# GpSimd waits for each group's own gathers in three stages of a graph network

## The reference

```python
# attention layer (twice): 8 heads of 16, then 1 head of 64
e = leaky_relu(xl[src] + xr[dst], 0.2)
logits = einsum('ehc,hc->eh', e, att)
m = segment_max(logits, dst, num_segments=N)
...
# third layer
pos_e = x_feat[src] + edge_attr
v = gelu(pos_e @ W1.T + b1, approximate=False) * bases
aggr = segment_sum(v, dst, num_segments=n_nodes)
```

## Time and profile before

| | us |
|---|---|
| median of 3 runs | 6841.29 |
| lowest and highest run | 6835.71, 6842.03 |
| span of the profiled execution | 8166.8 |

### The profile page before, as it was taken

How to read it: one execution, slowest core, us unless ns; L and a number is a source line. 1 busy time by engine, 2 the same in 40 slices (tenths; PEclk the granted TensorE clock), 3 DMA queues, 4 the chain that set the end, 5 groups by cost and what they waited for, 6 DMA issues and landing times. The chain is left out here.

```text
span 8166.8 us, 113382 instructions
## 1 busy us (share of the span) xinstructions
PE 6013.4 (74%) x30494; PEld 4713.9 (58%) x30494; DVE 3761.8 (46%) x13003; ACT 2160.8 (26%) x7007; POOL 4622.4 (57%) x4391
## 2 busy tenths in 40 slices
PE   3788878646766888876686887455555689989898
PEld 2666766535665666655575887355555544544545
DVE  5344443148973444311688335344555543333333
ACT  3222222228852222222697002111111220000000
POOL 2555555567865555555786552666666436366363
PEclk8666666768976666677898999677777789999999
DMA  5566654356642333323444664444444557867777
GB/s 202 180 188 207 206 177 130 109 93 142 140 78 69 79 77 80 73 61 60 63 76 73 238 228 154 116 128 126 127 128 127 107 178 261 291 230 265 262 263 239
DMA packets 904017, 1231.57 MB, mean 151 GB/s; under 512 B 230601, under 2 KB 640861, under 8 KB 890407
## 3 DMA queue, kind: packets, MB, share of 16 engines
q1 hardware_dynamic: 607544, 887.00, 34.1%
q0 software_dynamic: 207392, 219.55, 14.4%
q10 hardware_dynamic: 88428, 117.57, 4.2%
HBM read 987.45 MB, written 237.38 MB: 150 GB/s over the span
## 5 line engine op out<-in xcount | busy, mean ns | idle before, releaser
L1033 POOL DMA_INDIRECT ACC<-table,TABS x1760 | 1685.1, 957 | 1417.6 <-DMA kept<-ACC 814.0
L1348 POOL DMA_INDIRECT BUF<-table,TABS x840 | 795.3, 947 | 795.7 <-DMA table<-ACC 258.1
L1033 POOL DMA_INDIRECT BUF<-table,TABS x880 | 872.7, 992 | 554.4 <-issue 258.4
L1114 POOL DMA_INDIRECT adjacency<-TABS x600 | 966.9, 1611 | 303.2 <-issue 265.7
L1807 PE MATMUL picked<-ident,ACC 128*128 128x128 f32 (+1 forms) x3520 | 967.5, 364 | 156.7 <-issue 155.4
L1827 PE MATMUL lcol<-attT,BUF 128*128 128x8 f32 (+1 forms) x3520 | 619.6, 299 | 314.7 <-ACT BUF L1845 248.2
L1827 PEld LDWEIGHTS lcol<-attT,BUF 128*128 128x128 f32 (+1 forms) x3520 | 611.6, 259 | 399.1 <-issue 397.1
L1807 PEld LDWEIGHTS picked<-ident,ACC 128*128 128x128 f32 (+1 forms) x3520 | 727.4, 237 | 186.9 <-issue 186.8
L1806 PE MATMUL picked<-G,OH 128*128 128x128 f32 (+1 forms) x2352 | 680.0, 379 | 193.3 <-issue 178.6
L1819 DVE TENSOR_TENSOR BUF<-BUF,picked 128x512 f32<-128x512 f32 (+1 forms) x440 | 298.5, 679 | 1072.5 <-ACT BUF L1813 843.0
L1806 PEld LDWEIGHTS picked<-G,OH 128*128 128x128 f32 (+1 forms) x2352 | 472.9, 237 | 383.2 <-issue 362.9
(11 more groups left out here) (397 smaller groups left out, 10236.7 us busy)
## 6 DMA issues: line engine op xcount, KB each, us to landing
TABS<-adjacency SPq DMA_DIRECT2D x272, 512.0 KB
BUF<-in_edge_pair SPq DMA_DIRECT2D x880, 128.0 KB
BUF<-adjacency SPq DMA_DIRECT2D x102, 1024.0 KB
BUF<-adjacency SPq DMA_DIRECT2D x204, 512.0 KB
adjacency<-zeros ACTq DMA_DIRECT2D x44, 1792.0 KB
G<-adjacency SPq DMA_DIRECT2D x136, 512.0 KB
kept<-ACC SPq DMA_DIRECT2D x220, 272.0 KB
G<-kept SPq DMA_DIRECT2D x220, 272.0 KB
```

Source lines behind the costliest of these rows:

```text
L1033: po.indirect_dma_start(rows[:, slot, j, 0:width], None, tab, bass.IndirectOffsetOnAxis(ap=SRC[:, q * GT + j:q * GT + j + 1], axis=0)).the ...
L1114: po.indirect_dma_start(adj_flat, bass.IndirectOffsetOnAxis(ap=PLACE[:, k:k + 1], axis=0), TOTAL[:, k:k + 1], None, compute_op=ALU.add).th ...
L1348: po.indirect_dma_start(R[:, q % deep_ring, j, :], None, table, bass.IndirectOffsetOnAxis(ap=SRC[:, k:k + 1], axis=0)).then_inc(S(f"gather ...
```

## The change

`gather` gets one more line at its end: POOL waits until the four gathers that it has just issued have landed, and only then goes on with the next group. The wait is the same that PE (logit stages) and DVE (pair stage) already make before they use the rows. `gather` is called from the two logit stages and the pair stage, 660 times in all.

```diff
@@ -1033,6 +1033,7 @@
                 po.indirect_dma_start(rows[:, slot, j, 0:width], None, tab,
                                       bass.IndirectOffsetOnAxis(ap=SRC[:, q * GT + j:q * GT + j + 1], axis=0)
                                       ).then_inc(S(f"gathered{slot}"), 16)
+            gathered(po, q)
 
         def gathered(eng, q):
             eng.wait_ge(S(f"gathered{q % DEEP}"), 16 * GT * (q // DEEP + 1))
```

## The result

The changed kernel takes **8549.58 us** (median; 8540.41 to 8558.24), the kernel before 6838.5: a ratio of 1.251 (95% interval 1.250 to 1.253), or 1711 us more. The forecast was 8000, between 7070 and 8390. The sign and the mechanism were right; the time lies 550 us above the forecast and 160 above the range.

What follows compares the result with a forecast made beforehand. With the wait, POOL was to pace all three gather stages: 4.78 + 1.5 + 0.78 = 7.06 us a group against 5.30 before, times 660 = 1162 us on 6841, said as 8000 us, range 7070 to 8390.

Steps and rivals of the forecast that it cites:

- What bounds the kernel: Three gather stages: in the trace POOL is ahead by all 12 slots and something else sets the pace, 6.65 us a group.
- The hold: Gather stages: while a stream of gathers runs, PE's finished work reaches nobody until it lands; ACT's copies lose 409.6 us.
- Trace and runs differ: Placing the 1325.5 us between profile and runs: gather stages run at 5.3 us a group, between 5.08 and 5.55.
- Landing: Each group's end: data lands 1.5 us after the last gather's record ends, bounds 1.43 and 1.87.
- The signs of failure that I named: Fails if POOL stands much under 2.2 us a group, the span grows 260 us beyond the time, or slot waits stay.
- Restart: POOL after a release: next gather starts 0.78 us later, where a queued one needs 0.30.
- Four gathers with their gaps: POOL's issuing of one group, line 1033: four gathers and three 0.30 us gaps take 4.78 us on average.
- The lead of 12 slots hides nothing: Gather stages: POOL's lead, worth 64 us, hides latency, not rate, and is used up or never built within forty groups.
- One factor for everything: Rival, whole kernel: runs are the trace shortened by 0.838, gathers, landing and restart too; + 231, so 7072 us; chance 0.14.
- Faster: Rival, gather stages: the hold paces the runs too and the wait's pauses let PE's signals through; 6643 us, chance 0.06.
- No change: Rival, gather stages: the wait is covered, POOL's cycle stays within 0.02 us of the pace before; 6841 us, chance 0.04.
- What the profile was to show: Gather stages: about 660 POOL stands of 2.3 us, groups every 7.1 us, waits for `kept` and `sum_up` nearly gone.

Runs made afterwards that it cites:

- disturbed execution: The kernel before, unchanged, in the execution the prediction's profile shows: span 8166.8 us, 1.3 ms longer than its others, cause unknown; met once more at 8156.8 us.
- the kernel with swapped rows: Changed kernel, but groups 100 to 119 of each stage gather group 219's rows, and 213 to 219 group 100's: 8610.9 us beside 8542.2; 8908.1 in an earlier execution.
- the second wait: Changed kernel with another wait in each group, after its second gather: 9697.1 us, ratio 1.420; 10260 us was expected.

## Why the prediction was right or wrong

**What bounds the kernel.** Right in the place, wrong in the reason for this profile. "Something else sets the pace" held for the disturbed execution; undisturbed it is POOL, as shown by leaving out a quarter of its gathers. The hold itself was told too sharply. "What PE has finished reaches nobody" while gathers run, but in the very stream that starts at 5700.38 ACT's copy starts 0.04 us after the end of the transposes that it takes:

```profile
5703.84 1.06 PE L1666 MATMUL turned<-ident,BUF 128*128 128x128 f32 x4
5704.94 0.60 ACT L1673 ACTIVATE BUF<-turned 128x512 f32<-128x512 f32 x1 [1.22 <-issue]
```

So some of PE's signals got through and others did not until the stream had landed; which, and why, stays open.

**Trace and runs differ.** The pace before was to be 5.3 us, between 5.08 and 5.55. It is 5.10, at the lower end: the second of the two divisions that I worked out there (1037 us from the gather stages, 288 from the transfers) is what happened. From first gather to last the three stages of the two profiles differ by 4390 - 3365 = 1025 us (3365 from the starts above), the mixed and the last one by 103 and 230. The 350 GB/s for the transfers were too hopeful, since undisturbed they reach 291 and 299. Cost of the step: 0.20 x 660 = 132 us.

**Landing.** This is the step that failed. I took 1.5 us, with bounds of 1.43 and 1.87 from six releases, "near the low end, since the runs carry less delay than the trace everywhere else". The mean stand is 2.90 us; less 0.76 of restart that is a landing of 2.14 us, outside the bounds. So is logit stage 1 (3.12 - 0.76 = 2.36) and the pair stage (2.26), while logit stage 2, with the fewest transfers, has 1.79 and lies inside them. My 1.5 is near the landing at its shortest, as in this stretch of logit stage 2 after the change:

```profile
2925.67 0.95 POOL L1033 DMA_INDIRECT ACC<-table,TABS  x1 [2.27 <-DMA ACC<-table,TABS]
...
2939.70 0.95 POOL L1033 DMA_INDIRECT ACC<-table,TABS  x1 [2.33 <-DMA ACC<-table,TABS]
```

2.27 less 0.76 is 1.51; the shortest stand of that stage is 2.16 us, the median 2.34. In logit stage 1 the median is 2.60 and the mean 3.13, since one stand in ten is over 5.4. A wait that ends each group pays the mean, with its tail, and the runs name part of what is in it: three quarters of SP's fetches (0.54 us in the pair stage), the zero fills (0.45 us or a little more over the first 80 groups of logit stage 1) and the last groups' rows (4.24 instead of 2.94 us at the end of the pair stage). The argument that the undisturbed runs carry less delay was beside the point: the kernel with swapped rows has the same mean stand in the pair stage in either condition (3.17 us), so the delay of the disturbed profile was not in the landings. The signs of failure that I named looked only for a stand much shorter than 2.2 us, and it was longer. Cost of the step: (2.90 - 2.28) x 660 = 409 us.

The Trainium skill ("DMA: Bandwidth & Descriptors", Anatomy of one DMA — SWDGE (gpsimd) path) gives by its formula 2.15 us from a gather's issue to its landing, and my estimate from that was 7805 us for the kernel. The trace has 2.3 at the least and 2.6 in the median, so the measurement decides against it, more than against my own bounds.

**Restart.** 0.78 was right as a duration. (It was counted from the end of the instruction that released POOL, the 0.76 here from the start of the one that the same landing released.) But it is no price of a release: 0.58 of it goes when the slot wait and the increment stand ahead of the wait. It was read off a row and not taken apart. That did no harm to this forecast and makes 0.58 x 660 = 383 us of the 560 by which the one for the second wait was off.

**Four gathers with their gaps.** 4.78 against 7.73 - 2.90 = 4.83: 0.055 x 660 = 36 us. The gathers' means are the prediction's own (957 and 993 ns); what is new are the 33 gaps of 1.30 us, 33 us together. With 1162 + 132 + 409 + 36 = 1739 the sum meets the 1731.5 between the spans.

**The lead of 12 slots hides nothing.** Right, and shown by its reverse: looking one group back costs 26 us where looking at the own group costs 1711.

**The rivals.** One factor for everything: the undisturbed gather has the same 945 ns in the median as the earlier trace rows, so it falls. Faster: the hold is not there in undisturbed runs. In the disturbed condition it is, and there the change costs, by an estimate from single executions, 8908 - 69 (the swapped rows) - 8157 = 682 us and not 1711. So 1 ms comes back there, as this rival would have it, and the change still loses, since landing and restart are 2.9 us and not under 1.8. No change: falls with the stand.

**What the profile was to show.** 660 stands of 2.3 us, 1500 in all: 653 of 2.90, 1891. 7.1 us a group and 28 groups in 200 us: 7.73 and 26. The waits for `kept` gone: yes. Those for `sum_up` gone: in name no, in fact yes. The span was to be near 8430 in the condition of the first profile; by the kernel with swapped rows it is some 8906 - 69 = 8837, and what is missing, 407 us, is as much as the landing was short of.

## What to carry to other kernels

When a producer is the bound, a wait for its own last transfer costs its full latency and restart in every turn, and here a ring of 12 slots hid none of it; the same wait one group back cost 0.5%. Price such a wait at the mean of the stage with everything else that moves there, and not at the shortest row. If it must stay, put all bookkeeping of the queue ahead of it: moving it so gave back 497 us. And where a profile's span is far from the runs, first look at a stage that the change can't touch: transfers at 236 and 257 GB/s instead of 291 and 299 told here that the whole execution was another one.

## What the runs showed of the hardware

- In the disturbed condition the two streaming stages take 14 to 24% longer (1550 us instead of 1354 and 541 instead of 438 at the ends). The kernel with long unbroken streams of gathers loses 1 ms more there, and one with gathers in fours does not.
- A gather of 128 rows takes POOL 945 ns in the median, whether the rows are 256 or 512 bytes (logit stage 2 and 1).
- A gather that starts while DVE's L1701 runs takes 1.39 us at 0.12 us behind its start and 1.12 at 0.38. If the gather started first, both keep their lengths, 0.94 and 0.69 us.
- PE's busy time rose from 1025 to 1296 us in logit stage 1, and from 713 to 943 in the pair stage, for as many instructions. Its idle times between groups are longer, and its granted clock is 0.60 and 0.67 instead of 0.74 and 0.81, so more of the time is at its lower level, 1.2 GHz. It shows in no time here: POOL's stands and gathers make up the whole growth.
